# Two reorderings in the even batches of a four-layer fused kernel: a residual sum ahead of two masked minima on the vector engine, a mixing product ahead of the value products on the tensor engine

## The chip, the cores and the metric

The kernel runs on one core of a Trainium2 chip, as one launch. The metric is device time in microseconds (us), the median of several runs. Engines are named as in the profile: PE is TensorE (PEld its weight loads), DVE is VectorE, ACT is ScalarE, POOL is GpSimd, SP is SyncE, which here only issues transfers. The engines run their own instruction streams in order and meet at semaphores.

## The reference

Four layers with residual sums act on `x` of 64 batches x 64 tokens x 512 features, all in float32:

```
x = x + x @ W[id] + b[id]                      # L0: one of 16 weight matrices for each batch
x = x + x @ W.T + s * (x @ A.T) @ Bm.T         # L1: dense layer and one of 8 low-rank adapters
x = x + attention(x) @ Wo.T                    # L2: 8 query heads, 4 key groups, 64 wide, window of 256,
                                               #     keys and values in a paged cache that x's own rows
                                               #     are written to first
x = x + (w[subject].T @ x) + bias[subject]     # L3: 64 x 64 mixing of the token rows, per batch
```

In L3 the contraction runs over the 64 token rows of a batch, so the product is of a 64 x 64 matrix with a 64 x 512 tile. The output is the last `x`.

## The kernel before, in words

The program has two phases, one after the other. Phase one (the first half of the time) does L0, L1 and the query, key and value rows for 32 pairs of batches. It leaves `x2` (the stream after L1) in DRAM, pair by pair. Phase two does the attention and L3. The change is in phase two only.

Phase two is one loop over the batch b from 0 to 67, software-pipelined: each engine has its own function `phase_two(b, j, s)`, in which steps of several batches stand in a fixed order written out by hand. The order of the lines is the order of execution on that engine. On PE a step of batch b is, in this order:

- `scores(0)`, `scores(1)` of b (L630), which fill the two score banks;
- `transpose_keys` of b+1, first half (L608, L609);
- in an even b from 4 on: `project` second half (L670, six products), which ends `wo_done`;
- `transpose_probs` of b-1 (L640, L645), ten transposes, each bank of them then copied to SBUF: the first by DVE (`copy_first`, L1026), the second and the small third by ACT (L790, L795);
- `scores(2)`, `scores(3)` of b;
- `transpose_keys` of b+1, second half, which waits for ACT's copy of the first half (`kt_ready`, L767);
- in an odd b: `project` first half (L670, six products);
- `values()` of b-1 (L658, then L663 for the batch's own keys), which waits for the three copies and ends `pv_done`;
- in an even b from 4 on: the mixing product of L3 (L702) for the pair (b-4)/2. It waits for `x3_ready` and reads and writes the bank `ps_x`.

In the profile each of these float32 products is two matrix instructions, so "x2" at L702 is one product.

On DVE a step of batch b is: `masked(0)` and `masked(1)` (L1044: mask added to the scores, with their minimum, since the scores are negated, kept as `neg_max`); in an odd b the last sum with x3 that gives the output rows (`x4`, L1056); `copy_first` of b-1 (L1026); `masked(2)`, `masked(3)`; in an even b the sum with x2 that gives `x3` (L1066), which reads `ps_x` after `wo_done`; the reciprocal and the four scalings of the probabilities (L1071, L1074); the next mask (L1011, L1012); and `split_outputs` of b-1 (L1032), which waits for ACT's copy `ot_hi` (L816) of the value sums, which waits for `pv_done`. After it comes `masked(0)` of b+1.

ACT takes the exponentials of the four groups (L783), copies keys and probabilities, and at the end of its step copies the value sums (`ot_hi`, L816). POOL gathers the rows of the cache by indirect transfers (L449, L475, L486). In an odd batch SP, released by `x4`, stores an output pair and loads the next pair's x2 rows, mixing matrices and biases.

Of the kernel before, what the change touches and what calls it, by code (L numbers as in the profile page):

```python
# [12 lines left out]
NB, T, D = 64, 64, 512  # L13
# [36 lines left out]
def build(nc, a):  # L50

    ctx = ExitStack()
    with ctx:
# [161 lines left out]
        def loop(eng, step, slots, first, end, last):  # L215

            for n in range(first):
                step(n, n // slots, n % slots)
            with eng.Fori(first // slots, last // slots) as j:
                for s in range(slots):  # L220
                    step(j * slots + s, j, s)
            for n in range(last, end):
                step(n, n // slots, n % slots)

        def on(n, lag, count):

            return not isinstance(n, int) or 0 <= n - lag < count

        def wait(eng, semaphore, value):

            if not isinstance(value, int) or value > 0:
                eng.wait_ge(semaphore, value)
# [3 lines left out]
        def wait_alone(eng, name, semaphore, value):  # L236


            wait(eng, semaphore, value)
            if not isinstance(value, int):  # L240
                eng.sem_inc(waits_passed[name], 1)
# [258 lines left out]
        def _(pe):  # L500
# [114 lines left out]
            def phase_two(b, j, s):  # L615
# [32 lines left out]
                def values():  # L648

                    pe.wait_ge(pt0_ready, b)  # L650
                    pe.wait_ge(pt1_ready, b)
                    pe.wait_ge(pt2_ready, b)
                    wait(pe, ot_ready, b - 1)
                    for p in range(GP):
                        for c in range(2):
                            for q in range(2):
                                v0 = G * HD + (2 * p + q) * HD
                                nc.tensor.matmul(ps_o[HD * q:HD * q + HD, p * P:(p + 1) * P], kv[:, r, c, v0:v0 + HD], pt[:, p, q, c, :],  # L658
                                                 start=(c == 0 and p == 0), stop=False, skip_group_check=True)
                    for p in range(GP):  # L660
                        for q in range(2):
                            v0 = G * HD + (2 * p + q) * HD
                            last = nc.tensor.matmul(ps_o[HD * q:HD * q + HD, p * P:(p + 1) * P], kv[T * q:T * q + T, r, 2, v0:v0 + HD],  # L663
                                                    pt2[T * q:T * q + T, p, :], start=False, stop=(p == GP - 1), skip_group_check=True)
                    last.then_inc(pv_done, 1)

                def project(chunks):
                    for c in chunks:
                        for n, (o_part, w_part) in enumerate(((ot_hi, wo_hi), (ot_hi, wo_lo), (ot_lo, wo_hi))):
                            last = nc.tensor.matmul(ps_x[:, :], o_part[:, pair_s, c, :], w_part[:, c, :],  # L670
                                                    start=(c == 0 and n == 0), stop=(c == DC - 1 and n == 2))
                    return last
# [15 lines left out]
                if first_half:  # L688
# [4 lines left out]
                        pe.wait_ge(wo_lo_ready, 1)  # L693
                    wait(pe, x4_ready, pair)
                    project(range(DC // 2))
                if on(b, 1, NB):
                    values()
                if second_half:

                    pe.wait_ge(x3_ready, pair + 1)  # L700
                    pe.wait_ge(ld_pair[pair_s], PAIR_DMAS * 16 * (j * 2 + s // 4))
                    nc.tensor.matmul(ps_x[:, :], bd[:, pair_s, :], x3[:, pair_s, :], start=True, stop=True).then_inc(l3_done, 1)  # L702

            loop(pe, phase_two, KV_SLOTS, KV_SLOTS, NB + 3, NB - KV_SLOTS)


# [116 lines left out]
        def _(dve):  # L823
# [184 lines left out]
            def make_mask(b, s):  # L1008

                wait(dve, sm_ready, G * b - G)  # L1010
                V.tensor_copy(mask[:, s % 2, NK - 1:NK], beyond[:, bass.ds(b, 1)])  # L1011
                V.tensor_scalar(mask[:, s % 2, T:NK - 1], iota[:, 0:WIN - 1], first_key[:, bass.ds(b, 1)], BIG,  # L1012
                                ALU.is_lt, ALU.mult).then_inc(mask_ready, 1)
# [7 lines left out]
            def phase_two(b, j, s):  # L1021
                def copy_first():

                    dve.wait_ge(pt_done, 3 * b - 2)
                    wait(dve, pv_done, b - 1)
                    V.tensor_copy(pt[:, 0, :, :, :].rearrange("p q c t -> p (q c t)"), ps_pt[0][:, :]).then_inc(pt0_ready, 1)  # L1026

                def split_outputs():

                    dve.wait_ge(othi_ready, b)  # L1030
                    h, t = (s - 1) % 2, ((s - 1) % 4) // 2
                    V.tensor_tensor(ot_lo[:, t, :, T * h:T * h + T], ps_o[:, 0:2 * P].rearrange("p (c t) -> p c t", c=2 * GP),  # L1032
                                    ot_hi[:, t, :, T * h:T * h + T].bitcast(F32), ALU.subtract).then_inc(ot_ready, 1)


                added, finished = s % 2 == 0 and on(b, 4, NB), s % 2 == 1 and on(b, 5, NB)
                pair, pair_s = (b // 2 if isinstance(b, int) else j * 2 + s // 2) - 2, s // 2

                def masked(g):

                    dve.wait_ge(s_done, G * b + g + 1)
                    wait_alone(dve, "dve", e_ready, G * b + g - 2 * G + 1)
                    k0 = T * (1 - g % 2)
                    V.tensor_tensor_reduce(sm[:, s % 2, g, :], ps_s[g % 2][:, 0:NK], mask[:, s % 2, k0:k0 + NK], 1.0, 3.0e38,  # L1044
                                           ALU.add, ALU.min, accum_out=neg_max[:, s % 2, g:g + 1]).then_inc(sm_ready, 1)

                if on(b, 0, NB):
                    dve.wait_ge(mask_ready, b + 1)
                    masked(0)
                    masked(1)  # L1050
                if finished:

                    dve.wait_ge(l3_done, pair + 1)
                    dve.wait_ge(x3_ready, pair + 1)
                    wait(dve, st_out[pair_s], 16 * (j - 1))
                    V.scalar_tensor_tensor(x4[:, pair_s, :], ps_x[:, :], sbias[:, pair_s, 0:1], x3[:, pair_s, :],  # L1056
                                           ALU.add, ALU.add).then_inc(x4_ready, 1)
                if on(b, 1, NB):
                    copy_first()
                if on(b, 0, NB):  # L1060
                    masked(2)
                    masked(3)
                if added:
                    dve.wait_ge(wo_done, pair + 1)
                    dve.wait_ge(ld_pair[pair_s], PAIR_DMAS * 16 * j)
                    V.tensor_tensor(x3[:, pair_s, :], ps_x[:, :], x2_in[:, pair_s, :], ALU.add).then_inc(x3_ready, 1)  # L1066
                if on(b, 0, NB):

                    dve.wait_ge(e_ready, G * b + G)
                    wait(dve, prob_ready, G * b - G)  # L1070
                    V.reciprocal(recip[:, s % 2, :], row_sum[:, s % 2, :]).then_inc(recip_ready, 1)  # L1071
                    dve.wait_ge(recip_ready, b + 1)
                    for g in range(G):
                        V.tensor_scalar(prob[:, s % 2, g * NK:(g + 1) * NK], prob[:, s % 2, g * NK:(g + 1) * NK], recip[:, s % 2, g:g + 1], None,  # L1074
                                        ALU.mult).then_inc(prob_ready, 1)
                if on(b, -1, NB):
                    make_mask(b + 1, s + 1)
                if on(b, 1, NB):
                    split_outputs()

            loop(dve, phase_two, 4, 8, NB + 4, NB - 4)


# [71 lines left out]
```

## Time and profile before

| what | value |
|---|---|
| median of 3 runs | 1048.29 us (1042.13, 1048.29, 1052.52) |
| time of the profiled execution | 1051.5 us |
| its span, first to last instruction | 1049.7 us |
| PE busy | 962.4 us, 92% of the span |
| DVE busy | 618.0 us, 59% |
| POOL busy | 533.4 us, 51% |
| ACT busy | 387.2 us, 37% |
| mean granted TensorE clock | 0.978 of full |
| first L702, last L702 | 592.5 us, 1045.7 us |

Busy time of PE is from modelled ends of pipelined products, so 92% does not mean 92% of its peak. An idle time is shown in square brackets behind a row of the timeline, with what ended it. A releaser named "remote" is one that the profile could not name.

### The profile page before, as it was taken

What the parts mean: (1) busy time and instruction counts of PE and PEld (TensorE: products, weight loads), DVE (VectorE), ACT (ScalarE), POOL (GpSimd) and SP (SyncE); (2) the same over time, 40 slices, a digit from 0 to 9 for tenths busy, and PEclk for the clock granted to TensorE, in tenths of its full rate; (3) what the DMA queues carried; (4) which work ended last, traced back from release to release, by engine and by line L of the source; (5) the groups of instructions that cost most, each with busy time, mean ns of one, the idle gap of its engine ahead of it and who ended that gap; (6) DMA issues with size and microseconds to landing.
All of it is one profiled execution on the core that took longest, in us unless ns stands there. A gap on an engine that the chain in (4) does not pass through costs nothing.

```text
span 1049.7 us, 21785 instructions
## 1 busy us (share of the span) xinstructions
PE 962.4 (92%) x5891; PEld 646.8 (62%) x5891; DVE 618.0 (59%) x1772; ACT 387.2 (37%) x1061; POOL 533.4 (51%) x481
## 2 busy tenths in 40 slices
PE   2899999999999997999937999999999999999997
PEld 0566766676676665666624666666666666666664
DVE  3533334766676643355524677667666766776674
ACT  1221222122122211222114566565555545564662
POOL 1245455556545578655456555555455545555530
PEclk9999999999999999999966999999999999999999
DMA  8778888768767876768145565655565555555641
GB/s 261 240 256 276 296 276 271 236 224 267 253 233 237 265 236 195 249 230 286 60 135 167 167 185 160 186 170 179 153 183 160 167 186 177 170 168 180 185 131 42
DMA packets 106072, 212.53 MB, mean 202 GB/s; under 512 B 30827, under 2 KB 53224, under 8 KB 97586
## 3 DMA queue, kind: packets, MB, share of 16 engines
q1 hardware_dynamic: 70610, 145.54, 42.4%
q0 software_dynamic: 25408, 57.82, 19.3%
q10 hardware_dynamic: 10016, 8.73, 2.6%
q8 instruction: 15, 0.25, 0.1%
q14 instruction: 23, 0.19, 0.1%
HBM read 204.47 MB, written 33.86 MB: 227 GB/s over the span
## 4 chain that ended last, share of the span: by engine, by line
PE 31%; issue 11%; POOL 7%; ACT 5%; another core or an unknown queue 3%; DMA 2%; SPq 1%; DVE 1%; ACTq 1%; DVEq 0%; POOLq 0%
PE ps L670 6%; PE ps L630 6%; PE ps L658 5%; PE ps L640 4%; PE ps L663 3%; PE ps L608 3%; PE ps L702 3%; ACT big L783 2%; POOL rms L414 2%; ACT kt L767 1%; POOL table_i L397 1%; POOL ring L418 1%; DMA ring<-in_rope 1%; ACT pt L790 1%
## 5 line engine op out<-in xcount | busy, mean ns | idle before, releaser
L486 POOL DMA_INDIRECT ring<-new_rows,idx x128 | 132.1, 1032 | 131.6 <-DVE big L1074 66.6
L783 ACT ACTIVATE big<-big,neg_max 128x320 f32<-128x320 f32 x256 | 141.8, 555 | 120.9 <-DVE neg_max L1044 72.1
L1044 DVE CUSTOM_DVE_ANT_0 big<-ps,mask 128x320 f32<-128x320 f32 x256 | 115.7, 488 | 55.5 <-PE ps L630 34.5
L414 POOL TENSOR_TENSOR rms<-ss,neg_half 128x12 f32<-128x12 f32 x32 | 73.1, 2285 | 140.4 <-DVE ss L987 140.2
L511 PE MATMUL ps<-ring 128*64 128x512 f32 x512 | 118.9, 607 | 17.3 <-DMA ring<-in_w 17.3
L630 PE MATMUL ps<-kt,q_in 64*128 64x320 f32 x512 | 108.0, 491 | 0.7 <-DVE neg_max L1044 0.6
L728 ACT ACTIVATE x2t_hi<-ps 128x512 fp32r<-128x512 f32 x32 | 19.1, 597 | 230.4 <-PE ps L519 230.4
L511 PEld LDWEIGHTS ps<-ring 128*64 128x64 f32 x512 | 34.6, 138 | 96.9 <-issue 96.9
L404 POOL TENSOR_TENSOR x_in<-x_in,bias_in 128x512 f32<-128x512 f32 x32 | 41.9, 1309 | 93.2 <-DMA ring<-in_rope 93.1
L1074 DVE TENSOR_SCALAR big<-big,recip 128x320 f32<-128x320 f32 x256 | 85.6, 396 | 2.3
L475 POOL DMA_INDIRECT ring<-new_rows,idx x64 | 61.4, 959 | 49.8 <-PE ps L645 33.4
L658 PE MATMUL ps<-pt,ring 128*64 128x128 f32 x1024 | 70.9, 281 | 12.7 <-ACT pt L795 11.9
L449 POOL DMA_INDIRECT ring<-in_kvrows,idx x64 | 61.2, 956 | 41.1 <-issue 19.5
L608 PE MATMUL ps<-ident,ring 128*128 128x128 f32 x256 | 57.2, 306 | 22.8 <-DMA ring<-new_rows,idx 9.4
L608 PEld LDWEIGHTS ps<-ident,ring 128*128 128x128 f32 x256 | 26.2, 143 | 83.5 <-issue 67.6
L658 PEld LDWEIGHTS ps<-pt,ring 128*64 128x64 f32 x1024 | 55.9, 138 | 30.4 <-issue 29.3
L554 PE MATMUL ps<-wqkv_hi,x2t_hi 128*128 128x512 f32 x256 | 71.5, 423 | 2.0 <-ACT wqkv_hi L746 2.0
L755 ACT ACTIVATE sq<-ps 128x512 f32<-128x512 f32 x32 | 19.1, 597 | 145.0 <-PE ps L564 139.2
L956 DVE TENSOR_TENSOR x<-ps,x_in 128x512 f32<-128x512 f32 x32 | 22.1, 692 | 81.7 <-PE ps L511 81.7
L562 PE MATMUL ps<-wqkv_hi,x2t_lo 128*128 128x512 f32 x256 | 69.1, 392 | 0.1
L564 PE MATMUL ps<-wqkv_lo,x2t_hi 128*128 128x512 f32 x256 | 68.5, 389 | 0.0
L640 PE MATMUL ps<-ident,big 128*128 128x128 f32 x512 | 66.7, 273 | 0.0
(142 smaller groups left out, 1994.6 us busy)
## 6 DMA issues: line engine op xcount, KB each, us to landing
ring<-in_w SPq DMA_DIRECT2D x64, 1024.0 KB, 7.2
ring<-in_xt SPq DMA_DIRECT2D x32, 256.0 KB
x_in<-in_x SPq DMA_DIRECT2D x32, 256.0 KB
bias_in<-in_b SPq DMA_DIRECT2D x64, 128.0 KB
x_dram<-x SPq DMA_DIRECT2D x32, 256.0 KB, 5.4
q_dram<-q_t ACTq DMA_DIRECT2D x32, 256.0 KB
new_rows<-kv_out SPq DMA_DIRECT2D x32, 256.0 KB, 5.2
q_in<-q_dram SPq DMA_DIRECT2D x64, 128.0 KB
```

The source lines that it names most:

```text
L414: nc.gpsimd.tensor_tensor(rms[:, s, :], ss[:, s, :], neg_half[:, :], ALU.pow).then_inc(rms_ready, 1)
L486: pool.indirect_dma_start(out=kv[:, s, c, :], out_offset=None, in_=new_rows, in_offset=bass.IndirectOffsetOnAxis(ap=idx[:, b, 1 + c:2 + c] ...
L511: last = nc.tensor.matmul(ps_l0[T * h:T * h + T, :], xt[:, s, c, T * h:T * h + T], w0[:, 2 * s + h, c * D:(c + 1) * D], start=(c == 0), st ...
L554: nc.tensor.matmul(ps_out[:, :], x2t_hi[:, c, :], wqkv_hi[:, c, n0:n0 + D], start=(c == 0), stop=False)
L562: nc.tensor.matmul(ps_out[:, :], x2t_lo[:, c, :], wqkv_hi[:, c, n0:n0 + D], start=False, stop=False)
L608: nc.tensor.transpose(ps_kt[:, T + c * P:T + (c + 1) * P], kv[:, s, c, p * P:(p + 1) * P], ident[:, :])
L630: nc.tensor.matmul(ps_s[g % 2][:, 0:NK], q_in[r0:r0 + HD, s % 4, g // 2, :], kt[r0:r0 + HD, s % 2, g // 2, k0:k0 + NK], start=True, stop=T ...
L640: last = nc.tensor.transpose(ps_pt[p][:, (q * 2 + c) * P:(q * 2 + c + 1) * P], prob[:, r % 2, (5 * p + 3 * q + c) * P:(5 * p + 3 * q + c + ...
L658: nc.tensor.matmul(ps_o[HD * q:HD * q + HD, p * P:(p + 1) * P], kv[:, r, c, v0:v0 + HD], pt[:, p, q, c, :], start=(c == 0 and p == 0), sto ...
L783: nc.scalar.activation(prob[:, s % 2, g * NK:(g + 1) * NK], sm[:, s % 2, g, :], ACT.Exp, bias=neg_max[:, s % 2, g:g + 1], scale=-1.0, accu ...
L1044: V.tensor_tensor_reduce(sm[:, s % 2, g, :], ps_s[g % 2][:, 0:NK], mask[:, s % 2, k0:k0 + NK], 1.0, 3.0e38, ALU.add, ALU.min, accum_out=ne ...
L1074: V.tensor_scalar(prob[:, s % 2, g * NK:(g + 1) * NK], prob[:, s % 2, g * NK:(g + 1) * NK], recip[:, s % 2, g:g + 1], None, ALU.mult).then ...
```

## The change

In an even batch DVE takes the sum that gives `x3` right behind `copy_first`, ahead of `masked(2)` and `masked(3)`. PE takes the mixing product of L3 right behind the second half of `transpose_keys`, ahead of `values()`. No instruction is added or removed, and no wait is changed. In an odd batch neither engine has such a step. Line numbers behind the moved lines shift: L702 becomes L700 and L1066 becomes L1063.

```diff
@@ PE, phase_two
-                if on(b, 1, NB):
-                    values()
                 if second_half:
 
                     pe.wait_ge(x3_ready, pair + 1)
                     pe.wait_ge(ld_pair[pair_s], PAIR_DMAS * 16 * (j * 2 + s // 4))
                     nc.tensor.matmul(ps_x[:, :], bd[:, pair_s, :], x3[:, pair_s, :], start=True, stop=True).then_inc(l3_done, 1)
+                if on(b, 1, NB):
+                    values()
@@ DVE, phase_two
                 if on(b, 1, NB):
                     copy_first()
-                if on(b, 0, NB):
-                    masked(2)
-                    masked(3)
                 if added:
                     dve.wait_ge(wo_done, pair + 1)
                     dve.wait_ge(ld_pair[pair_s], PAIR_DMAS * 16 * j)
                     V.tensor_tensor(x3[:, pair_s, :], ps_x[:, :], x2_in[:, pair_s, :], ALU.add).then_inc(x3_ready, 1)
+                if on(b, 0, NB):
+                    masked(2)
+                    masked(3)
```

PE in batch 4, from its third score product to the first scores of batch 5, before (a product is one row here; `bias_in` is the buffer of x3, `ps` any PSUM bank):

```order
L630 MATMUL ps<-kt,q_in 128x320 [waits kt_ready,sm_ready]
L630 MATMUL ps<-kt,q_in 128x320 [waits sm_ready]
L608 MATMUL ps<-ident,ring 128x128 [waits kt_ready]
L608 MATMUL ps<-ident,ring 128x128
L609 MATMUL ps<-ident,ring 128x2x64
L658 MATMUL ps<-pt,ring 64x128 [waits pt2_ready,ot_ready,pt1_ready,pt0_ready]
L658 MATMUL ps<-pt,ring 64x128 x7
L663 MATMUL ps<-pt,ring 64x128 x4
L702 MATMUL ps<-bias_in,bd 128x512 [waits ld_pair0,x3_ready]
L630 MATMUL ps<-kt,q_in 128x320 [waits ld_q1,kt_ready,sm_ready]
```

And the same piece of the changed kernel:

```order
L630 MATMUL ps<-kt,q_in 128x320 [waits kt_ready,sm_ready]
L630 MATMUL ps<-kt,q_in 128x320 [waits sm_ready]
L608 MATMUL ps<-ident,ring 128x128 [waits kt_ready]
L608 MATMUL ps<-ident,ring 128x128
L609 MATMUL ps<-ident,ring 128x2x64
L700 MATMUL ps<-bias_in,bd 128x512 [waits ld_pair0,x3_ready]
L658 MATMUL ps<-pt,ring 64x128 [waits pt2_ready,ot_ready,pt1_ready,pt0_ready]
L658 MATMUL ps<-pt,ring 64x128 x7
L663 MATMUL ps<-pt,ring 64x128 x4
L630 MATMUL ps<-kt,q_in 128x320 [waits ld_q1,kt_ready,sm_ready]
```

The mixing product has moved from behind the value products to ahead of them, with its wait for x3.

DVE in the same batch, from the copy of the first probabilities to the reciprocal, before (L1044 is two rows, the masked minimum and the reading of its result; `big` holds the masked scores and the probabilities):

```order
L1026 COPY pt<-ps 128x512 [waits pv_done,pt_done]
L1044 ISA big,neg_max<-ps,mask 128x320 [waits e_ready,s_done]
L1044 ISA neg_max 128x1
L1044 ISA big,neg_max<-ps,mask 128x320 [waits e_ready,s_done]
L1044 ISA neg_max 128x1
L1066 TENSOR_TENSOR bias_in<-ps,x_in 128x512 [waits ld_pair0,wo_done]
L1071 RECIPROCAL recip<-row_sum 128x4 [waits prob_ready,e_ready]
```

And of the changed kernel:

```order
L1026 COPY pt<-ps 128x512 [waits pv_done,pt_done]
L1063 TENSOR_TENSOR bias_in<-ps,x_in 128x512 [waits ld_pair0,wo_done]
L1044 ISA big,neg_max<-ps,mask 128x320 [waits e_ready,s_done]
L1044 ISA neg_max 128x1
L1044 ISA big,neg_max<-ps,mask 128x320 [waits e_ready,s_done]
L1044 ISA neg_max 128x1
L1071 RECIPROCAL recip<-row_sum 128x4 [waits prob_ready,e_ready]
```

The sum that gives x3 has moved ahead of the two masked minima and their waits for scores. The streams of ACT, POOL and SP are the same row for row.

## Rows read from the trace of the kernel before

**Rows 1.** The page, busy time by engine.
```profile
PE 962.4 (92%) x5891; PEld 646.8 (62%) x5891; DVE 618.0 (59%) x1772; ACT 387.2 (37%) x1061; POOL 533.4 (51%) x481
```

**Rows 2.** Busy time in three stretches: length, then busy us (instructions) of each engine, clock.
```profile
600.00:740.00 140.00, 136.41 (x1057) 91.55 (x1052) 100.25 (x344) 82.88 (x248) 74.60 (x76) 1.00 0.60 177
740.00:890.00 150.00, 139.95 (x1067) 94.54 (x1063) 103.24 (x351) 80.31 (x250) 77.48 (x78) 1.00 0.56 169
890.00:1030.00 140.00, 134.46 (x1040) 90.03 (x1037) 100.07 (x343) 81.08 (x246) 65.08 (x66) 1.00 0.54 160
```

**Rows 3.** Groups of PE from 595 to 1030 us: busy, mean | idle before, releasers.
```profile
L658 PE MATMUL ps<-pt,ring 128*64 128x128 f32 x928 | 63.5, 278 | 8.0 <-ACT pt L795 7.2 <-issue 0.8
...
L608 PE MATMUL ps<-ident,ring 128*128 128x128 f32 x230 | 50.3, 300 | 10.6 <-issue 6.4 <-ACT kt L767 4.0
```

**Rows 4.** Waits from 560 to 1040 us: total us, times, longest.
```profile
DVE recip L1071 <- ACT big L783: 34.5, 51, 1.6
...
PEld ps L702 <- issue: 5.3, 31, 0.2
```

**Rows 5.** Timeline of PE, even batch: start, length, row, [idle before].
```profile
814.55 0.27 PE L609 MATMUL ps<-ident,ring 128*128 128x128 f32 x1
815.23 1.09 PE L658 MATMUL ps<-pt,ring 128*64 128x128 f32 x16 [0.40 <-ACT pt L795]
...
816.84 1.12 PE L702 MATMUL ps<-bias_in,bd 128*128 128x512 f32 x2
817.89 0.81 PE L630 MATMUL ps<-kt,q_in 64*128 64x320 f32 x4
```

**Rows 6.** Timeline of DVE, same batch.
```profile
814.34 0.49 DVE L1044 CUSTOM_DVE_ANT_0 big<-ps,mask 128x320 f32<-128x320 f32 x1 [0.80 <-PE ps L630]
...
815.47 0.69 DVE L1066 TENSOR_TENSOR bias_in<-ps,x_in 128x512 f32<-128x512 f32 x1
...
818.98 0.49 DVE L1044 CUSTOM_DVE_ANT_0 big<-ps,mask 128x320 f32<-128x320 f32 x1 [0.57 <-PE ps L630]
```

**Rows 7.** Timeline of PE, an even batch of the first stretch.
```profile
692.54 0.27 PE L609 MATMUL ps<-ident,ring 128*128 128x128 f32 x1
692.74 1.09 PE L658 MATMUL ps<-pt,ring 128*64 128x128 f32 x16
```

**Rows 8.** Timeline of DVE, same batch.
```profile
692.61 0.49 DVE L1044 CUSTOM_DVE_ANT_0 big<-ps,mask 128x320 f32<-128x320 f32 x1 [0.72 <-PE ps L630]
...
696.11 0.42 DVE L1032 TENSOR_TENSOR ot_lo<-ps,ot_hi 128x256 fp32r<-128x256 f32 x1
```

**Rows 9.** Timeline of ACT, copies of value sums (even, odd, odd, even batch).
```profile
695.01 0.38 ACT L816 ACTIVATE ot_hi<-ps 128x256 fp32r<-128x256 f32 x1 [0.29 <-PE ps L663]
...
732.25 0.38 ACT L816 ACTIVATE ot_hi<-ps 128x256 fp32r<-128x256 f32 x1 [1.19 <-PE ps L663]
...
811.18 0.38 ACT L816 ACTIVATE ot_hi<-ps 128x256 fp32r<-128x256 f32 x1 [3.12 <-remote]
...
817.16 0.38 ACT L816 ACTIVATE ot_hi<-ps 128x256 fp32r<-128x256 f32 x1 [0.54 <-PE ps L663]
```

**Rows 10.** Timeline of PE, odd batches.
```profile
731.41 0.65 PE L663 MATMUL ps<-pt,ring 64*64 64x128 f32 x8
...
733.01 0.27 PE L609 MATMUL ps<-ident,ring 128*128 128x128 f32 x1
733.03 0.48 PE L670 MATMUL ps<-wo_hi,ot_hi 128*128 128x512 f32 x1
...
808.79 0.65 PE L663 MATMUL ps<-pt,ring 64*64 64x128 f32 x8
```

**Rows 11.** Timeline of the last batches.
```profile
1036.75 0.68 DVE L1066 TENSOR_TENSOR bias_in<-ps,x_in 128x512 f32<-128x512 f32 x1
...
1037.71 1.09 PE L658 MATMUL ps<-pt,ring 128*64 128x128 f32 x16 [0.95 <-ACT pt L795]
...
1041.38 0.47 PE L670 MATMUL ps<-wo_hi,ot_hi 128*128 128x512 f32 x1 [0.94 <-DVE x L1056]
```

## The prediction, on record before the result

> **What bounds the kernel now.** I read the page first, for the engines' shares. PE is busy for 92% of the span, DVE for 59%, ACT for 37% [rows 1]. The change moves steps of phase two, so the next view is busy time by stretch. In the 430 us from 600 to 1030 us PE is idle for 3.6, 10.1 and 5.5 us of 140, 150 and 140 us [rows 2], 19.2 us together, at full clock. PE's stream sets the pace nearly everywhere; an order of work can only give back what lies in those 19.2 us, or lengthen them.
>
> The same rows show two rhythms. The first stretch passes 1057 PE instructions in 140 us, or 7.55 in a us; the second 1067 in 150, or 7.11. At the pace of the first, the second would take 141.3 us and the third 137.7: a slow rhythm costs 8.7 and 2.3 us. A pair of batches has 32 instructions of L658, so the 928 of rows 3 are 29 pairs of about 109 PE instructions: 14.4 us in the fast rhythm, 15.3 in the slow, and 11.0 us at 0.9 are 12 slow pairs.
>
> Third, the groups of PE: of its idle time 8.0 us lie ahead of the value products, nearly all waiting for ACT's small copy of probabilities [rows 3]. The timelines show where. In an even batch the transposes of keys end at 814.55 + 0.27 = 814.82, the value products start at 815.23 after 0.40 of idle time, then comes the mixing product, and 1.05 later the scores of the next batch [rows 5]. In an odd batch six projection products stand ahead of the value products and cover that wait (their first: [rows 10]). In the fast rhythm the even batch has no such gap: 692.54, then 692.74 [rows 7].
>
> **The change, part by part.** First, the product moved into the gap. It takes 816.84 to 817.89, 1.05 us [rows 5], longer than 0.40, so it covers the gap if x3 is there in time. DVE is free from 814.34 - 0.80 = 813.54 [rows 6]. The sum takes 0.69 [rows 6], so x3 is there at 814.23 and the product can start at 814.82: 0.6 us to spare. `wo_done` came one set of transposes earlier. In the fast batch DVE is free at 692.61 - 0.72 = 691.89 and x3 is ready at 692.58, just ahead of the keys' end [rows 8, 7]. Gain: the 8.0 us of rows 3; at 0.40 to 0.50 each they are some 18 even batches of the 29. Where x3 comes late, PE waits in turn. I put 0.6 us on that, two batches of 0.3; bounds are 0 and 0.3 in ten batches, 3 us.
>
> Second, changes of array shape on PE. Keys (128*128) to value products (128*64) takes 0.20 us from start to start [rows 7], keys to a product of the same shape 0.02 [rows 10]; weight loads of the mixing product behind the 64*64 products wait 5.3 us in 31 times, 0.17 each [rows 4]. Now the order of shapes is 128, 128, 64, 64, scores rather than 128, 64, 64, 128, scores. The gain is between 0 and 0.17 a batch, so between 0 and 5.3 us. I take 0.1, since the product's own exit into another shape stays, and only in the 18 batches that have a gap: 1.8 us. The Trainium skill, TensorEngine Tiling (Array Packing), section Key Properties, says that changing the tiling mode drains TensorE. By that rule one of four drains goes in each even batch; the 0.17 us agree with it. By the rule alone every even batch would gain the whole 0.17, 4.9 us for the 1.8, and the sum below would be -6.7.
>
> Third, the sum on DVE. Ahead of `masked(2)` DVE idles 0.80 or 0.72 [rows 6, 8], which hides 0.69. Behind `masked(3)` it covered a wait for the exponentials: the reciprocal waits 34.5 us in 51 times [rows 4]. That wait grows by what is taken from it; nothing is gained, nothing lost. Where the idle time is short the minima start up to 0.4 later; that goes into the probabilities, which PE needs only in the next batch.
>
> Fourth, what is delayed: the value sums. With the product ahead of them they end 1.05 later, less the filled gap and the saved shape change. They release ACT's `ot_hi`, that DVE's split, and behind the split stands `masked(0)` of the odd batch, which opens the chain minima, exponentials, key copy, transposes. Slow batch: the value products now start at 814.82 - 0.1 + 1.05 = 815.77, 0.54 later. ACT's copy goes from 817.16 [rows 9] to 817.70, ends at 818.08, the split takes 0.42, and `masked(0)` can start at 818.5. The scores now start at 817.39 and `masked(0)` needs them for 1.09 (817.89 to 818.98 [rows 5, 6]), so 818.48. The two meet: nothing is lost, but there is no reserve either. Fast batch: sums 0.96 later, ACT's copy from 695.01 [rows 9] to 695.97, its end 696.35, the split 696.4 instead of 696.11 [rows 8], and `masked(0)` behind it as much later: 0.3 us lost. In the 11 batches without a gap that is 3.3 us, bounds 0 (the copy's signal comes sooner) and 3.3. In the 18 with a gap I put 0.1, 1.8 us, with bounds 0 and 0.4, that is 7.2 us.
>
> Fifth, the end. In batch 64 there are no scores or minima. x3 is ready at 1037.43, the product would hold PE to about 1038.5, and the value products start there, not at 1037.71 [rows 11]. Their sums are 0.8 later. The next projection starts at 1041.38 after 0.94 of waiting for `x4` [rows 11]; the mixing product comes earlier now, but `x4` stands behind the split on DVE: 1038.5, value products 1.61 (815.23 to 816.84), copy 0.38, split 0.42, `x4` about as long as x3's 0.68, together 1041.6, and some 0.3 for three hand-overs. Cost 0.5.
>
> Nothing changes in the transfers or in POOL's stream. POOL's gathers wait for probabilities and transposes that move by less than 0.4, and each fills a buffer that is read three batches on.
>
> **The sum.** -8.0 - 1.8 + 0.6 + 3.3 + 1.8 + 0.5 = -3.6 us. With all bounds on the good side -8.0 - 5.3 + 0.5 = -12.8; on the bad side -8.0 + 3 + 3.3 + 7.2 + 0.5 = +6.0. The profiled execution took 1051.5 us, 3.2 above the median of the runs. Against it the sum gives 1047.9, and on the median's scale 1048.3 - 3.6 = 1044.7, so **1045 us**.
>
> **Rivals.** (a) The gap is filled and given back. The meeting point at 818.5 has no reserve, and a few tenths of lateness in `masked(0)` lengthen the next wait for keys by as much. For it: ACT's copy starts 1.93 us behind the start of the value products in the slow batch (815.23, 817.16) but 2.27 behind in the fast one (692.74, 695.01) [rows 5, 7, 9], so its signal can come 0.3 late. Against it: in an odd batch of the fast rhythm, where the sums are followed by scores as they now would be, it starts at 732.25 [rows 9], 0.2 behind their end at 731.41 + 0.65 [rows 10]. The time is then between 1048 and 1052: 1050.
>
> (b) Slower: the late signal. In the slow rhythm's odd batches the sums end at 808.79 + 0.65 = 809.44 [rows 10], yet ACT starts at 811.18, with a releaser that has no name [rows 9], 1.7 us later. There the sums are followed by scores. In the even batches the mixing product follows, and the lag is 0.3 (816.84 to 817.16 [rows 5, 9]). If the new order gives even batches the odd ones' lag, ACT's copy starts at about 819.15 and `masked(0)` at 819.95, not 818.98: +0.97 us a pair over now, in the 12 slow pairs +11.6. The other 17 lose 0.3, 5.1 us, and the end 0.5: +17.2, 1065. It decides as soon as the lag exceeds 0.3 us. Against it: fast odd batches have the same order and no lag.
>
> (c) The slow rhythm goes. It fills one stretch and hardly touches the first; the new order shifts the value sums against the transfers. If it goes, 8.7 + 2.3 = 11.0 us are saved, with the gaps outside it (8.0 less 0.4 in each of 12) 3.2 more, less the 0.5 at the end: -13.7, 1035. For it: that the first stretch does without. Against it: the change touches no transfer.
>
> **Chances.** My sum 0.55, (a) 0.22, (b) 0.11, (c) 0.12. A measurement of this kernel tells about 1%, 10.5 us, from no change: below 1037.8 is faster, above 1058.8 slower. Faster: (c) nearly whole and the low edge of my sum, 0.16. Slower: (b), 0.10. Within 1%: 0.74. The range takes my sum's bounds (1035.5 to 1054.3) and (a), leaves out (b) and about half of (c): 1035 to 1055.
>
> **What would show it.** Step one: idle time ahead of L658 between 595 and 1030 us falls from 8.0 to under 1, and L700 starts within 0.1 of the keys' end. If L700 waits for x3 in more than a few batches, step one's timing is wrong. Step two: starts of the keys' last transpose and of L700 lie within 0.1. Step three: the reciprocal's wait grows by about 0.6 in even batches. Step four: `masked(0)` of odd batches is released by ACT's copy or the split, no longer by scores, and the idle time ahead of L608 is about as before (10.6 us [rows 3]; 15.7 with my loss terms of 3.3 and 1.8, more is (a)). Rival (b): rows of L816 released by "remote" in even batches. Rival (c): the three stretches run at one pace, 7.5 instructions in a us. I am wrong if L608's idle time swallows the 8.0 us, or if the number of slow pairs moves by more than five.

## The result, and the profile after

The changed kernel takes 1036.8 us, the kernel before 1049.9 us in the same 22 rounds (medians, 13.1 us apart). The ratio, which leaves out one slow run of each kernel, is 0.9909, with a 95% interval of 0.9886 to 0.9932. That is -9.6 us of 1049.9, and this figure is used below. The forecast was 1045 us, -3.6 us. A second session (e6 below) gave 0.9948 [0.9909, 0.9988]. The profiled execution of the changed kernel spans 1034.9 us, the one before 1049.7.

Where the 14.8 us between the two spans lie is read from one landmark in both: the start of the value products of batch 4, and of batch 64. First the kernel before, timeline of PE:

```profile
590.94 1.09 PE L658 MATMUL ps<-pt,ring 128*64 128x128 f32 x16 [0.41 <-ACT pt L795]
```

and the changed kernel, the same and the end (start, length, row, [idle before]):

```profile
585.94 1.09 PE L658 MATMUL ps<-pt,ring 128*64 128x128 f32 x16
...
1021.62 1.09 PE L658 MATMUL ps<-pt,ring 128*64 128x128 f32 x16
...
1024.99 0.47 PE L670 MATMUL ps<-wo_hi,ot_hi 128*128 128x512 f32 x1 [1.69 <-DVE x L1056]
...
1026.74 0.63 PE L670 MATMUL ps<-wo_hi,ot_lo 128*128 128x512 f32 x1
```

The loop between the landmarks takes 435.7 us where it took 1037.71 - 590.94 = 446.8 [rows 11]: -11.1. The end takes 1034.9 - 1021.6 = 13.3 us where it took 12.0: +1.3. The mixing product of the pair stands behind this landmark before and ahead of it after, which matters for the end (fifth step, below). The remaining -5.0 lie ahead of batch 4, in phase one for the most part, whose code is the same; in the profiles of this study's kernels with that same code the first mixing product starts anywhere from 573.9 us (e3) to 592.5 us (before).

Busy time of the changed kernel by stretch, columns as in [rows 2]:

```profile
600.00:740.00 140.00, 136.17 (x1071) 92.41 (x1070) 101.28 (x349) 82.93 (x251) 75.65 (x77) 1.00 0.59 176
740.00:890.00 150.00, 144.66 (x1118) 98.17 (x1119) 105.87 (x366) 87.12 (x262) 79.58 (x82) 1.00 0.61 179
890.00:1020.00 130.00, 126.10 (x985) 85.78 (x983) 93.67 (x322) 77.87 (x233) 58.58 (x60) 1.00 0.53 158
```

The paces are 7.65, 7.45 and 7.58 PE instructions in a us; they were 7.55, 7.11 and 7.43. The first stretch is 1.3% faster, and the middle one has lost most of its lag. Counted from one mixing product of L3 to the next, 18 of the first 28 pairs took more than 14.8 us in the kernel before (14.83 to 16.50), and 3 do in the changed one (15.39, 15.50 and 15.99). The 28 pairs together took 420.3 us and take 409.6.

Groups of PE from 595 to 1018 us, beside [rows 3]:

```profile
L658 PE MATMUL ps<-pt,ring 128*64 128x128 f32 x928 | 63.5, 279 | 0.2 <-ACT pt L795 0.2
...
L608 PE MATMUL ps<-ident,ring 128*128 128x128 f32 x228 | 49.9, 300 | 11.3 <-issue 9.9 <-ACT kt L767 1.2
...
L700 PE MATMUL ps<-bias_in,bd 128*128 128x512 f32 x58 | 30.8, 612 | 0.4 <-issue 0.4
```

The gap ahead of the value products fell from 8.0 to 0.2 us; the mixing product waits 0.4, and the keys' idle time rose only from 10.6 to 11.3. One even batch, PE, beside [rows 5] and [rows 7]:

```profile
685.79 0.27 PE L609 MATMUL ps<-ident,ring 128*128 128x128 f32 x1
685.89 1.02 PE L700 MATMUL ps<-bias_in,bd 128*128 128x512 f32 x2
686.85 1.09 PE L658 MATMUL ps<-pt,ring 128*64 128x128 f32 x16
...
688.46 0.81 PE L630 MATMUL ps<-kt,q_in 64*128 64x320 f32 x4
```

From the start of the last key transpose to the next scores it takes 2.67 us. A batch of before without a gap took 0.20 to the value products [rows 7] and then, as in [rows 5], 816.84 - 815.23 = 1.61 to the mixing product and 1.05 to the scores: 2.86. The new order saves 0.19 where x3 is in time.

Last, the hand-over that my fourth step feared. In another even batch of the changed kernel, DVE and then ACT:

```profile
808.00 0.42 DVE L1032 TENSOR_TENSOR ot_lo<-ps,ot_hi 128x256 fp32r<-128x256 f32 x1
808.45 0.49 DVE L1044 CUSTOM_DVE_ANT_0 big<-ps,mask 128x320 f32<-128x320 f32 x1
```
```profile
807.38 0.38 ACT L816 ACTIVATE ot_hi<-ps 128x256 fp32r<-128x256 f32 x1 [0.76 <-PE ps L663]
```

The value products had started at 805.65 in that timeline, so the copy starts 1.73 us behind them; it was 1.93 in the slow and 2.27 in the fast batch of before [rows 5, 7, 9]. The copy ends at 807.76 and the split starts 0.24 later, held by DVE's own work and not by the copy.

### The profile page after: what moved, and what is told of

It reads as the page before. It is cut to its first block, busy times and chain, and to the rows that moved or that the text cites. A ratio compares the mean times of both kernels' runs of the same rounds, so it can differ in the third digit from the quotient of the medians.

```text
span 1034.9 us, 21785 instructions
## 1 busy us (share of the span) xinstructions
PE 957.3 (93%) x5891; PEld 646.3 (62%) x5891; DVE 606.4 (59%) x1772; ACT 391.5 (38%) x1061; POOL 530.1 (51%) x481
## 4 chain that ended last, share of the span: by engine, by line
PE 41%; issue 15%; POOL 14%; DMA 14%; SPq 13%; ACT 2%; another core or an unknown queue 1%; DVE 0%; POOLq 0%; ACTq 0%; DVEq 0%
DMA ring<-in_rope 13%; PE ps L630 8%; PE ps L670 8%; PE ps L658 6%; PE ps L640 5%; PE ps L608 4%; POOL x_in L404 4%; PE ps L663 4%; PE ps L700 3%; POOL rms L414 3%; SPq L267 3%; POOL ring L433 2%; SPq L262 2%; SPq L269 2%; POOL ring L418 2%
## 5 line engine op out<-in xcount | busy, mean ns | idle before, releaser
L486 POOL DMA_INDIRECT ring<-new_rows,idx x128 | 130.3, 1018 | 132.6 <-DVE big L1074 71.9
L1044 DVE CUSTOM_DVE_ANT_0 big<-ps,mask 128x320 f32<-128x320 f32 x256 | 116.1, 488 | 44.9 <-PE ps L630 23.5
L404 POOL TENSOR_TENSOR x_in<-x_in,bias_in 128x512 f32<-128x512 f32 x32 | 44.9, 1404 | 149.5 <-DMA ring<-in_rope 149.3
L1074 DVE TENSOR_SCALAR big<-big,recip 128x320 f32<-128x320 f32 x256 | 83.2, 388 | 2.3
L554 PE MATMUL ps<-wqkv_hi,x2t_hi 128*128 128x512 f32 x256 | 69.3, 413 | 2.0 <-ACT wqkv_hi L746 2.0
```

The source lines that it names most:

```text
L404: nc.gpsimd.tensor_tensor(xb[:, s, :], x_in[:, s, :], bias_in[:, s, :], ALU.add).then_inc(xb_ready, 1)
L486: pool.indirect_dma_start(out=kv[:, s, c, :], out_offset=None, in_=new_rows, in_offset=bass.IndirectOffsetOnAxis(ap=idx[:, b, 1 + c:2 + c] ...
```

## The experiments

The kernel before took 1047 to 1051 us in the sessions of the two results above (the second is that of e5 to e8) and some 1028 us in those of e1 to e4 and of e9 to e12. These three sessions of experiments ran on three different chips, one each, so that the runs can't tell the session from the chip. Each ratio is to runs of the kernel before in the same session.

**e1: the sum on DVE alone.**

```diff
 PE:  values(); mixing product            # as before
 DVE: copy_first(); x3; masked(2); masked(3)
```

> Only the DVE sum that gives x3 is moved ahead of the third and fourth masked minimum; the mixing product stays behind the value products. Theory A (the gain is PE's: the product fills the wait for ACT's copy, and the sum on DVE is hidden on either side): 0 us, between -1 and +2, so about 1050, and the 8.0 us of idle time ahead of the value products stay. Theory B (the sum delayed the reciprocal and with it the chain of the next batch): a good part of the 9.6 us gained, 1043 or less, with the idle time ahead of the value products unchanged.

Measured: ratio 1.0007 [0.9977, 1.0036]. Theory A's number, and not B's. But its trace has no gap ahead of the value products at all, where theory A said 8.0 us would stay. All of PE's idle time from 595 to 1010 us, and PE in a pair of batches:

```profile
PE ps L608 <- ACT kt L767: 7.5, 26, 0.4
```
```profile
716.78 0.27 PE L609 MATMUL ps<-ident,ring 128*128 128x128 f32 x1
716.98 1.09 PE L658 MATMUL ps<-pt,ring 128*64 128x128 f32 x16
...
718.59 1.13 PE L702 MATMUL ps<-bias_in,bd 128*128 128x512 f32 x2
719.64 0.81 PE L630 MATMUL ps<-kt,q_in 64*128 64x320 f32 x4
...
723.04 0.44 PE L608 MATMUL ps<-ident,ring 128*128 128x128 f32 x2 [0.28 <-ACT kt L767]
```

The mixing product before this one started at 704.12, so a pair takes 14.47 us here. Nearly all do (14.2 to 14.6), and the only wait is of 0.28 us for keys in the odd batch.

**e2: the mixing product alone.**

```diff
 PE:  mixing product; values()
 DVE: copy_first(); masked(2); masked(3); x3   # as before
```

> Only the mixing product is moved ahead of the value products; DVE gives x3 behind the fourth masked minimum as before. Theory A: the product waits for x3, which in the slow batch of before is there at 816.2 and not at 814.8, so the scores of the next batch start 1.0 us later than before, in a fast batch 1.4 us: +28 to +40 us, 1078 to 1090, with the idle time ahead of the mixing product at 1.3 us in each of 29 batches. Rival: the wait is absorbed by work that is off the bound elsewhere: under +15 us.

Measured: 1069.1 us against 1027.7, ratio 1.0435 [1.0384, 1.0486], +44.7 us. PE's waits from 595 to 1010 us:

```profile
PE ps L700 <- DVE bias_in L1066: 37.5, 27, 1.4
PE ps L608 <- ACT kt L767: 5.3, 25, 0.2
```

27 waits of 1.4 us each: theory A by mechanism, and 5 us over its upper end. The move on PE needs the one on DVE. What the move on DVE is worth alone is known only from these runs near 1028 us, where both together are worth nothing either (e4 and e9 below). In a session near 1048 us, where theory B would have to show, it was not run.

**e3 and e4: a later copy of the value sums in even batches**, ahead of `ot_hi` in the kernel before (e3) and the changed one (e4).

```diff
+                    if s % 2 == 0:
+                        nc.scalar.activation(spare[:, :], ps_o[:, 0:2 * P], ACT.Copy)
                     nc.scalar.activation(ot_hi...
```

> The kernel before, with one more copy of the value sums on ACT (0.38 us, into a buffer nobody reads) ahead of ot_hi in the even batches. By the rows of before the split on DVE has 0.3 us or more to spare in these batches: 0 to +3 us, 1050 to 1053. If the hand-over of the value sums already bounds it, +0.38 in 32 pairs, +12 us.

> The changed kernel with the same extra copy on ACT ahead of ot_hi in the even batches. My forecast said that the change leaves this hand-over no reserve: then each 0.38 us shows, +11 us over the changed kernel, 1048 to 1051. By the changed kernel's trace (copy at 807.38, split at 808.00, held by DVE's own work) the reserve is 0.2 us: +0.18 in 29 pairs, +5 us, about 1042 to 1045. If the hand-over is off the bound altogether, no change: 1037 to 1040.

Measured: e3 1.0001 [0.9973, 1.003], e4 1.0008 [0.9976, 1.004]. e3 is as expected. For e4 the absolute numbers don't apply, since the kernel before took 1027.7 on that chip. Its neighbour e9 (the changed kernel but for one DVE step, same base of 1027.8) has 1.0013. The pairs tell it more finely than the ratios: the first 28 take 405.2 us in e4 and 404.9 in e9, and 405.0 in e3 and in e1. So the added copy costs 0.3 us at most, where "no reserve" meant +11 us and a reserve of 0.2 us meant +5. The hand-over in even batches is off the bound, in a session without late hand-overs; in one with them this was not run.

e3 also says why e1 has no gap. Its order is the old one on both engines, and its waits from 595 to 1010 us are:

```profile
PE ps L609 <- ACT kt L768: 7.5, 26, 0.4
PE ps L659 <- ACT pt L796: 0.9, 1, 0.9
```

The gap is away without the move on DVE too (the one wait of 0.9 us is that of batch 64), so it is the session that has none, and not e1's order. e11 below, the old order again, shows the same.

**e5 and e6: both kernels again.** No edit.

> The kernel before, run again, for a trace from this chip. In the trace of before that the forecast used, ot_hi started 1.7 us late in a dozen odd batches; in the traces of the first four experiments, from another chip, the sum-only variant had no such case and no gap ahead of the value products, although it was as fast as the kernel before there. Theory C (the late hand-overs, and with them the gaps, come with the chip or the run and not with the kernel): the gap ahead of the value products is either there in many batches together with late rows of ot_hi, or absent with them. Ratio 1.000.

> The changed kernel again. Theory C: if the trace of before from this chip has the late hand-overs, the ratio is 0.985 to 0.995 as in the first result; if it has none, there is no gap to fill, only the change of array shape is saved (0.1 to 0.2 us in 29 batches, if the pace follows PE) against 1 us at the end: ratio 0.996 to 1.001. Theory A alone (the gap is a property of the order): 0.99 on any chip.

Measured: e5 1.0051 [1.0001, 1.0101], e6 0.9948 [0.9909, 0.9988]. The unchanged kernel came out at the edge of its own interval, so the ratios of e5 to e8 are good to about half a per cent. What released ACT's copy `ot_hi` over the whole run (us, times), and PE's largest waits from 595 to 1010 us, in e5:

```profile
  remote: 49.9, 16
  PE ps L663: 38.2, 41
```
```profile
PE ps L658 <- ACT pt L795: 9.2, 20, 1.3
PE ps L608 <- ACT kt L767: 6.9, 19, 0.5
PE ps L608 <- issue: 5.3, 22, 0.5
```

and in e6:

```profile
  PE ps L663: 60.9, 59
  remote: 6.3, 2
```
```profile
PE ps L608 <- issue: 8.1, 25, 0.5
...
PE ps L658 <- ACT pt L795: 0.4, 1, 0.4
```

In the first traces the same line had 11 copies released by "remote" before and 3 after. e1, in the other session, has 33 released by L663 and none by "remote". No trace of the sessions near 1028 us names "remote" in this loop, on any engine. So the late hand-overs come with the session, as theory C has it.

Not every gap stands behind a late copy, though. From the first mixing product on, 11 of the 18 gaps of the first trace do, and 15 of the 21 of e5. Most of the others stand behind another late hand-over of an odd batch, that of the third scores to DVE's minimum (L1044), 5 of 7 and 4 of 6. The kernel before, DVE and then PE, and the changed kernel, DVE:

```profile
641.75 0.49 DVE L1044 CUSTOM_DVE_ANT_0 big<-ps,mask 128x320 f32<-128x320 f32 x1 [1.90 <-remote]
...
648.89 1.09 PE L658 MATMUL ps<-pt,ring 128*64 128x128 f32 x16 [0.41 <-issue]
```
```profile
827.25 0.49 DVE L1044 CUSTOM_DVE_ANT_0 big<-ps,mask 128x320 f32<-128x320 f32 x1 [1.88 <-remote]
```

L1044 was released by "remote" in this way, before and then changed, both first traces (us, times):

```profile
  remote: 8.2, 6
```
```profile
  remote: 15.8, 14
```

In the second session it is 4 times before and 7 times in e6. So the changed kernel has few late copies (3 and 2, against 11 and 16), but not fewer late hand-overs in the first trace: 17 of both kinds in either kernel, and 20 against 9 in the second session. They fall elsewhere, and cost less there. A pair with a late minimum and its copy in time takes 14.2 to 14.6 us in the changed kernel's first trace, where such pairs took 14.85 to 15.30 before, with a gap; that is the gap filled. A pair with a late copy takes 15.5 or 16.0 us, and took 15.2 to 16.5 before. And in the kernel before late copies come in runs: the pair that starts at 738 us has one, and so has each of the next eight (nine in e5, from 734 us on). In the changed kernel and in e6 the pair at the same place (730 and 734 us) has one, and the next have none. Why the new order breaks such a run is not shown.

**e7 and e8: every odd hand-over late**, in the kernel before and in the changed one.

```diff
+                    if s % 2 == 1:
+                        for i in range(6):
+                            nc.scalar.activation(spare[:, i, :], ps_o[:, 0:2 * P], ACT.Copy)
                     nc.scalar.activation(ot_hi...
```

> The kernel before, with six more copies of the value sums on ACT ahead of ot_hi in every odd batch (some 1.6 us, into a buffer nobody reads). It forces in all pairs what the late signal did in a dozen: masked(0) of the even batch late, keys late, a gap of 0.4 us ahead of the value products. By the rhythms of before +0.9 us in 29 pairs: +26 us, or a ratio near 1.025; idle time ahead of the value products about 12 us between 595 and 1030 us.

> The changed kernel with the same six copies. Theory A with C: the mixing product fills the gap in every pair, so this is faster than the kernel before with the six copies by 0.4 (gap) and 0.1 to 0.2 (shape) in 29 pairs, 14 to 17 us: ratio near 1.010. Rival: the split after the even batch bounds it, as my forecast's fourth step had it, and only half or less of this is left: ratio 1.018 or more.

Measured: e7 1106.4 us, ratio 1.0549 [1.0466, 1.0631]; e8 1060.8 us, ratio 1.016 [1.0087, 1.0232]. The order that was before loses 57 us by late odd hand-overs, twice what I expected; the changed order loses 22 us against e6. PE's waits from 595 to 1010 us, e7:

```profile
PE ps L631 <- DVE neg_max L1048: 23.0, 19, 2.2
...
PE ps L659 <- ACT pt L796: 8.5, 20, 0.8
```

and e8 (lines are one higher than in the kernels without the copies):

```profile
PE ps L609 <- issue: 14.0, 39, 0.5
...
PE ps L631 <- DVE neg_max L1048: 5.7, 4, 2.2
```

Lateness opens the gap ahead of the value products (8.5 us here and 11.5 up to 1095 us, 12 expected), and the changed order closes it. But the lateness is not the same in the two. What released the first of the six copies (L819), in e7 and then in e8:

```profile
  remote: 40.7, 13
  PE ps L664: 33.6, 17
```
```profile
  PE ps L664: 26.5, 22
  remote: 10.4, 3
```

The session's own late hand-overs come on top of the added ones. In e7 `ot_hi` starts 1.6 to 1.9 us behind the end of the value sums in 9 of 30 odd batches, as intended, and 2.5 to 4.4 us behind in 21; in e8 1.6 to 2.2 us in 27 and 3.2 to 4.4 us in 3. The further 21 cost most: their pairs take 16.2 to 19.5 us, and all 19 waits of the third scores for a masked minimum (L631) are in such pairs. Of the pairs with the added lateness alone, eight in e7 take 15.4 us in the mean and 26 in e8 15.15, so that the changed order saves some 0.25 us in such a pair, where 0.5 to 0.6 was expected. By this estimate some 7 of the 46 us between the two kernels' first 28 pairs (478.2 and 432.5 us) are the order's direct gain; the rest comes with the further late hand-overs, of which the changed order has fewer here as in e6. e7's granted clock was also down to 0.95 to 0.98 from 600 to 1010 us, where e8's is 0.99 to 1.00; this part is not isolated.

**e9: x3 one step earlier still.**

```diff
 DVE: x3; copy_first(); masked(2); masked(3)   # on the changed kernel
```

> The changed kernel with the sum that gives x3 one step earlier still, ahead of copy_first. In the changed kernel's trace the weight load of the mixing product waits for x3 in 7 batches, 4.2 us, most of it at the end of the loop, and PE idles 0.4 us for it. If x3 bounds anything there, 1 to 3 us come off; by the trace it does not: within 1 us of the changed kernel, ratio to before 0.990 to 0.995 on a chip with late hand-overs. If the copy of the first probabilities, now 0.7 later, opens a new gap ahead of the value products, +0.3 in 29 pairs, ratio near 1.000.

Measured: 1.0013 [0.9977, 1.0049], in a session of 1027.8 us, so the trace tells more than the ratio. PE:

```profile
701.80 0.27 PE L609 MATMUL ps<-ident,ring 128*128 128x128 f32 x1
701.91 1.02 PE L700 MATMUL ps<-bias_in,bd 128*128 128x512 f32 x2
702.86 1.09 PE L658 MATMUL ps<-pt,ring 128*64 128x128 f32 x16
...
708.05 0.44 PE L608 MATMUL ps<-ident,ring 128*128 128x128 f32 x2 [0.47 <-ACT kt L767]
```

Beside e1: the even batch is 0.19 us shorter, the wait for keys in the odd batch went from 0.28 to 0.47, and with the next mixing product at 716.38 a pair takes 14.47 us again. The saved change of array shape is handed to the next wait in full.

**e10: the odd batches' projection ahead of the key transposes.**

```diff
 PE, odd batch, on the changed kernel:
-  transpose_keys(b + 1, ..., 1); project(range(DC // 2)); values()
+  project(range(DC // 2)); transpose_keys(b + 1, ..., 1); values()
```

> The changed kernel with, in the odd batches, the six projection products ahead of the second half of the key transposes and not behind them, so that they cover the wait for ACT's key copy (most of the 11 us of idle time ahead of L608). Theory A: the same trick as the one studied, worth 0.2 to 0.3 us in 29 odd batches: 6 to 8 us less than the changed kernel, ratio to before near 0.984 on a chip with late hand-overs. Rival: the keys are transposed 1.5 us later and ACT's copy of them delays the next batch: no gain or a loss of up to 0.3 in 29 batches.

Measured: 1013.1 us against 1027.8, ratio 0.9875 [0.9833, 0.9917]. Busy time of its first two stretches:

```profile
600.00:740.00 140.00, 140.00 (x1106) 96.56 (x1104) 104.47 (x361) 85.77 (x260) 78.69 (x81) 1.00 0.61 183
740.00:880.00 140.00, 140.00 (x1103) 96.65 (x1102) 104.70 (x361) 85.75 (x260) 78.55 (x81) 1.00 0.62 187
```

PE has no idle time left in these two stretches, and the pace is 7.90 instructions in a us. It fills the wait that e1 and e9 show: the first 28 pairs take 391.8 us, 13.1 less than in e9. Against e9 the ratios give some 14 us, twice the 6 to 8 expected, since the wait is some 0.47 us in nearly every pair here, and not 0.2 to 0.3.

**e11: without the mixing loads.** The kernel before, with the loads of L3's matrices and biases left out from the third pair on, so that its later outputs are not the reference's. The two waits for these loads are lowered to match.

```diff
-                    for h in range(2):
+                    for h in range(2 if isinstance(k, int) and k < 2 else 0):
```

> The kernel before, without the loads of mixing matrices and biases of L3 from the third pair on (the buffers keep those of the first two pairs); the loads of x2 stay. Theory D: the late hand-overs of the odd batches come from these many small transfers, which SP issues just then: on a chip where before takes about 1048 us, the late rows of ot_hi in odd batches go from 11 or 16 to 2 or fewer, the gap ahead of the value products goes, and 8 to 15 us come off, ratio 0.986 to 0.992. Rival: they come from the gathers or from something else: rows and time as before, ratio 0.997 to 1.003. On a chip where before takes about 1028 us it tells nothing.

Measured: 1.0001 [0.997, 1.0033], in a session of 1027.8 us. On the loads it tells nothing, as said: a session without late hand-overs can't show their cause, and that stays open. As a trace of the old order it bears out e1 and e3: its only wait from 595 to 1005 us is PE's for keys, 7.6 us in 26 times, and there is no gap ahead of the value products.

**e12: three steps together.**

```diff
 DVE: as e9;  PE, odd batches: as e10
 PE, batch 64: values(); mixing product        # the old order, there alone
```

> The changed kernel with x3's sum ahead of copy_first, the odd batches' projection ahead of the key transposes, and in batch 64 alone the old order, value products ahead of the mixing product (there PE waited 1.7 us for x4 in the changed kernel's trace, against 0.9 before). The three add up if each holds: the odd batches' 6 to 8 us, and 1 to 2 us at the end, 8 to 10 us less than the changed kernel, ratio near 0.981. If the odd batches' part fails, within 2 us of the changed kernel.

Measured: 1012.8 us, ratio 0.9868 [0.9827, 0.9909], the same as e10 within the intervals. It is faster than the kernel before, by 13.6 us, and than the changed kernel's nearest neighbour of that session (e9), by some 15, where 8 to 10 were expected; the gain is e10's step. The other two steps add nothing that the time shows, although the wait for x4 in batch 64 is back at 0.9 us from e10's 1.7.

## Why the prediction was right or wrong

The forecast had the sign, and the time lies in its range; the size was 3.6 against 9.6 us. By its own steps, on the traces of before and after:

- First step, the gap: -8.0 forecast, 8.0 to 0.2 measured, -7.8. x3's lateness: +0.6 forecast, +0.4 measured, and +1.9 in e6. e2 shows that this rests on the sum's move.
- Second step, the array shape: -1.8 forecast with -5.3 as its bound. The loop became 11.1 us shorter. PE's idle time between the same landmarks went from 20.2 to 13.8 us, which explains 6.4, and the remaining 4.7 us are 0.16 in each of 30 pairs, against 0.19 in the batch shown. I had counted it only in batches with a gap, since I took the batches without one to be bound by DVE. In the 1028 us sessions that is what happens (e9). The rule of the Trainium skill on changes of tiling mode (TensorEngine Tiling (Array Packing), Key Properties) agrees with the 0.19 us that PE saves in a batch, and says nothing of the loop's time.
- Third step, the sum on DVE: 0 forecast, 1.0007 in e1, in a session without gaps. The reciprocal's wait grew from 34.5 to 49.5 us, about 0.5 in an even batch, as the step had it.
- Fourth step, the later value sums: +5.1 us forecast, +0.7 measured. **This is the step that failed most.** It moved ACT's copy by as much as the sums were moved, kept its lag behind them, and let DVE's split wait for it. In the even batch shown the lag behind the start of the sums is 1.73 us and not 2.27, and the split waits for DVE's own work. e4 shows 0.38 us more on that path costing nothing, in a session without late hand-overs. Why the lag fell is not shown; over 28 even batches its median behind the end of the sums is 0.52 us in the trace of before, 0.13 in that of after, and 0.20 in e1, whose order on PE is the old one. I had a short lag in hand, the odd batch's 0.2, and used it only in a rival.
- Fifth step, the end: +0.5 forecast. Read from the last transpose of probabilities in batch 64, with the same work behind it in both orders, the end takes 13.3 us before, 15.4 in the changed kernel and 13.9 in e6:

```profile
1036.38 0.38 PE L645 MATMUL ps<-ident,big 128*128 128x128 f32 x2
```
```profile
1019.46 0.38 PE L645 MATMUL ps<-ident,big 128*128 128x128 f32 x2
```

  That is +2.1 and +0.6. PE's wait for x4 grew from 0.94 to 1.69 us in both. The other 1.6 us of the first are the clock (last section) and not the order, so the step was about right.

Of the rivals, (a) is refuted near 1048 us by the 11.3 us, (b) by the even batches: from the first mixing product on no copy there is released by "remote", in any of the four traces. (c), given 0.12, is in good part what happened in the sessions near 1048 us: the slow rhythm went. I had priced its whole disappearance at -13.7. I had also named as a sign of being wrong that the number of slow pairs moves by more than five, and it went from 18 (not the 12 that I had worked out from the paces) to 3, and from 20 to 3 in the second session. So the sum names the right places and prices most of them, but it took the rhythm as given, and the rhythm is what changed.

What the forecast left out is that before's profile was of a disturbed rhythm. Its 8.0 us of gaps were taken as a property of the order; e1, e3 and e11 show the old order on PE without any. The first 28 pairs take, in us:

| order on PE | near 1048 | near 1028 |
|---|---|---|
| old | 420.3 (before), 424.6 (e5) | 405.0 (e1), 405.0 (e3), 405.2 (e11) |
| new | 409.6 (changed), 409.9 (e6) | 405.2 (e4), 404.9 (e9) |

The disturbance costs the old order 15 to 20 us and the new one 5, and without it the new order gains nothing. The forecast was read from a disturbed trace and met a disturbed session; in one near 1028 us its -3.6 us would have met no gain. That its sign came out is to this extent luck. The changed kernel itself was not timed near 1028 us, only these two neighbours. What delays the hand-overs of the odd batches, and why the changed order has fewer late copies, is not settled; without that, a good share of the -11.1 us has a place but no first cause.

## What to carry to other kernels

An in-order engine that stops for a copy can take any product whose inputs are ready ahead of the stop; its producer on the other engine has to move as well, or the wait is bought dearly (e2, +4.4%). Look for the wait that is left in every period and fill that one: e10 filled 0.3 to 0.5 us a pair with work that stood right behind it. A gap that comes and goes along one trace, while the code is the same, says that the order is sensitive to something late, and its filling is worth what that lateness is worth in the run at hand.

## What the runs showed of the hardware that was not expected

- The same kernel took 1047 to 1051 us in two sessions and 1028 us in two others, at a mean granted clock of 0.98 in the traces of either sort but for two of 0.99. The traces near 1048 have value sums whose copy starts late, by a releaser without a name, while PE goes on starting products: mostly 1.6 to 1.9 us behind the modelled end of the last product, and once in each trace 2.8 to 3.2 us (4.2 us of idle time ahead of the one in before). Masked minima come late behind their scores in the same way. The eight traces near 1028 name no such releaser in this loop.
- Behind 1.69 us of idle time on PE, of twelve products of one shape the first four started 0.24 to 0.35 us apart, the next seven 0.43 us behind one another, and the last 0.31. The granted clock ahead of and in that stretch (columns as in [rows 2]):

```profile
1023.40:1025.40 2.00, 0.41 (x2) 0.39 (x3) 1.08 (x2) 0.33 (x1) 0.00 (x0) 1.00 0.00 0
1025.90:1028.80 2.90, 2.90 (x8) 2.30 (x7) 0.00 (x0) 0.00 (x0) 0.00 (x0) 0.50 0.18 69
```

  It is 0.50, the lower of its two levels (1.2 and not 2.4 GHz). In the kernel before, PE idled for 0.94 us there and the same products ran at 1.00. In e6, the same program as the changed kernel, PE idled for the same 1.69 us and the products stayed 0.23 apart, at 1.00. So the idle time alone does not decide it. Of the seven traces with an idle time of 1.7 to 2.0 us there, three have such a fall (the changed kernel, e4 and e10); of the seven with 0.9 none has. The products take 1.6 us longer from first to last than in e6 (4.20 against 2.65), which is what the first trace's end lost more than e6's.
